# Cross-attention and FFN on one core: the first pair of heads scored in front of the last value tile, the first batch's transposes behind the next keys, the first keys chunk by chunk

## The chip, the cores and the metric

One Trainium2 chip, of which the kernel uses one core. The metric is the device time of one execution in microseconds (us); a run is compared with runs of the kernel before on the same chip.

## The reference

For each of B = 4 batches, x is 512 rows by 512 columns, and a context has T = 1601 rows of 512. The kernel computes, in float32:

```
q = layernorm(x) Wq^T + bq        k = ctx Wk^T + bk        v = ctx Wv^T + bv      (16 heads of 32)
p = softmax(clip(q k^T / sqrt(32), -50, 50)), masked rows of the context count as -50
a = LN((clip(rs, 0, 0.3) * (p v Wo^T + bo))) * gamma + beta;     x1 = x + a
y = fwht(layernorm(x1) * SU_ug) ; g = silu(y Wgate^T) * (y Wup^T) ; out = x1 + fwht(g * SU_dp) Wdown^T
```

## The kernel before

All instructions are written out per engine in hand-made order, with semaphores between the engines: each engine runs its own list, and a wait holds up everything behind it in that list. Large products are made from two fp32r parts of each operand, a high part (a copy, on ScalarE) and a low part (the difference, on VectorE), with three matmuls for each chunk of 128 rows of the contraction (`split_product`, L132).

**Stages.** `context` (L689) goes through the four batches. For each it first makes keys and values of the 1601 context rows in six pieces (`NP`, `FROM`: tiles of 128 rows, two per piece and three in the last, 13 in all), and then the scores and the attention, 52 steps. `ffn` follows. A piece is: load of the raw context (SyncE), its high part `split_hi` (L677, ScalarE) and low part `split_lo` (L682, VectorE); `keys` (L1187, TensorE), four tiles of 48 matmuls in all; `keys_hi` (L883) and `keys_lo` (L1030), which take each key tile out of its PSUM bank; `weighted` (L1196), the value products, 12 matmuls for each tile of context rows; `values_out` (L905), ScalarE's copy of a value tile into `vt`. Keys and values share the four banks `kv` = both halves of `sc[0]` and `sc[1]` (L711), so value tile i waits for the low part of key tile i, and the next piece's keys wait for the value copies.

**The first batch** also makes the queries of all four batches, one at a time (class `Queries`, L524): `norm` (L601, VectorE, with `root` on ScalarE), `transposes` (L625, TensorE, 16 matmuls of 128 columns), `rows_hi` and `rows_lo` (L576, L612), `project` (L634, 48 matmuls) and `query_hi` and `query_lo` (L585, L617). These use the other four banks, `banks` = both halves of `sc[2]`, `acc` and `tot` (L712). On TensorE (L1286 to L1305) piece p does keys(p), project(p - 1), weighted(p), transposes(p). On ScalarE (`first_piece` L953, `query_piece` L965) it does rows_hi, keys_hi, root, query_hi, values_out; on VectorE (L1097, L1107) rows_lo, keys_lo, norm, in piece 1 the first half of the butterflies of the down weights (`butterfly_ahead`, L489), query_lo, and in piece 1 the other half. SyncE loads (`first`, L784); GpSimd loads and stores the output, up and gate weights (L856 to L869) when the third and fourth transposes are done.

In front of everything TensorE waits (L1283) for the low parts of all four chunks of the key weights (`weights_lo`, L596). ScalarE makes the high part of the second context piece (L958) before it takes the first key tiles.

**The turn.** When the last value tile (tile 12, 65 rows) is copied into `vt`, `scores(b, 0)` (L1204) begins: 12 matmuls of 32 rows by 512 columns for four heads, three for each head, four heads side by side. Step i makes two pairs of heads, n = 2i and 2i + 1, each in a bank `sc[n % 3]` of two halves. `exps` (L930, ScalarE) takes the exponential of one pair at a time, `clips` (L1083, VectorE) bounds it, `values` (L1216) multiplies with `vt`, `sums` (L1228) adds up. `scores(b, i)` waits until all but the last exponential of the step before are done (L1207), since there are three banks for two pairs a step. The queries of batches 2 to 4 are loaded back from DRAM (`query`, L756) and must be there before the first scores; so must the low parts of the rotated rows (`rotated_lo`, L376), which use the banks of `sc[2]`. In the first batch, before the first exponential, ScalarE also waits for the stores of the output, up and gate weights (L1022, L1023), whose space the probabilities take.

## Time and profile before

| | us |
|---|---|
| median of three runs | 1475.78 (1474.55 to 1476.06) |
| the profiled execution, its own time | 1475.65 |
| span of its instructions | 1473.8 |
| TensorE busy | 1424.8 (97%) |
| VectorE busy | 1108.7 (75%) |
| ScalarE busy | 815.1 (55%) |
| mean granted TensorE clock | 0.989 of full speed |

The profiled execution's time is 1.85 us more than its span; times in timelines count from the span's start. PE is TensorE's matmuls, PEld its weight loads, DVE VectorE, ACT ScalarE, POOL GpSimd, SP SyncE. Busy times of matmuls run to their modelled ends, so that a row's length holds a tail beyond the start of the next instruction.

### The profile page before, as it was taken

Reading aid. Unit: us, or ns where it says so; the run is one execution under the profiler, and the core shown is the slowest. Engines: PE = TensorE matmul, PEld = TensorE weight load, DVE = VectorE, ACT = ScalarE, POOL = GpSimd, SP = SyncE. Lnnn points to the kernel's source line nnn. Section 1 sums busy time; section 2 is a strip of 40 time slices with the busy share of each in tenths; the row PEclk is TensorE's granted clock in tenths of the full one; section 3 lists DMA queues with packets and bytes.
Section 4 is the critical chain, followed back from the end, with each engine's and each line's share of the span. In section 5 each row is a group of like instructions: output and inputs, shape, how many; then the busy total and the mean of one; then the engine's idle time right before and its main releaser. Section 6 shows DMA issues by size and latency. Waiting matters only on the chain. (4 is left out here: it accounts for less than half of the span.)

```text
span 1473.8 us, 25109 instructions
## 1 busy us (share of the span) xinstructions
PE 1424.8 (97%) x10352; PEld 955.6 (65%) x10352; DVE 1108.7 (75%) x1657; ACT 815.1 (55%) x1018; POOL 88.9 (6%) x128
## 2 busy tenths in 40 slices
PE   5999999999999999999999999998999999999997
PEld 5887333688333688333588333576788888888886
DVE  5953899895899885799885799887765565656554
ACT  4343899535899635899634899534432333333330
POOL 1000000101000100000100000110010010000100
PEclk9999999999999999999999999999999999999999
DMA  8453000436100425100424500362345544455435
GB/s 270 149 189 143 9 10 10 148 104 203 79 17 10 138 84 192 36 17 10 137 79 179 226 16 10 95 236 84 143 150 203 189 173 146 157 205 178 171 143 171
DMA packets 54785, 180.91 MB, mean 123 GB/s; under 512 B 11168, under 2 KB 25760, under 8 KB 42384
## 3 DMA queue, kind: packets, MB, share of 16 engines
q1 hardware_dynamic: 39696, 116.08, 21.9%
q0 software_dynamic: 14976, 63.23, 12.7%
q8 instruction: 82, 1.34, 0.4%
q14 instruction: 31, 0.25, 0.1%
HBM read 111.97 MB, written 67.31 MB: 122 GB/s over the span
## 5 line engine op out<-in xcount | busy, mean ns | idle before, releaser
L944 ACT ACTIVATE cx_probs<-cx_sc,proj_mbias 128x1024 f32<-128x1024 f32 (+1 forms) x416 | 442.7, 1114 | 45.7 <-PE cx_sc L1211 38.1
L1089 DVE TENSOR_SCALAR cx_probs<-cx_probs 128x1024 f32<-128x1024 f32 (+1 forms) x416 | 269.9, 684 | 57.1 <-ACT cx_probs L944 55.7
L1051 DVE TENSOR_TENSOR cx_padd<-cx_probs,cx_probs 128x1024 f32<-128x1024 f32 x192 | 233.6, 1217 | 1.1 <-DVE cx_probs L1089 0.2
L1211 PEld LDWEIGHTS cx_sc<-cx_q,cx_kt 32*128 32x128 f32 (+1 forms) x2496 | 103.6, 183 | 198.3 <-ACT cx_probs L944 181.3
L1224 PE MATMUL cx_acc<-cx_probs,cx_vt 128*32 128x512 f32 (+1 forms) x1664 | 220.9, 603 | 3.7 <-DVE cx_probs L1089 3.7
L1211 PE MATMUL cx_sc<-cx_q,cx_kt 32*128 32x512 f32 (+1 forms) x2496 | 206.5, 433 | 14.5 <-ACT cx_probs L944 11.1
L136 PE MATMUL cx_sc<-proj_cs,proj_wk 128*128 128x256 f32 (+1 forms) x1152 | 149.1, 289 | 11.1 <-DVE proj_wk L599 11.1
L136 PEld LDWEIGHTS cx_sc<-proj_cs,proj_wk 128*128 128x128 f32 x1152 | 145.4, 190 | 15.3 <-issue 14.2
L136 PE MATMUL cx_sc<-proj_wv,proj_cs 128*128 128x512 f32 (+1 forms) x624 | 149.6, 396 | 1.2 <-DVE cx_kt L1036 1.2
L136 PE MATMUL ff_yp<-hand_wds,ff_held 128*128 128x512 f32 x624 | 147.9, 395 | 0.1
L1686 DVE TENSOR_TENSOR ff_x<-ff_yp,ff_x 128x512 f32<-128x512 f32 x128 | 85.6, 689 | 75.0 <-PE ff_yp L136 62.1
L136 PEld LDWEIGHTS ff_yp<-hand_wds,ff_held 128*128 128x128 f32 x624 | 117.1, 188 | 28.8 <-DVE ff_kept L1749 0.5
L136 PEld LDWEIGHTS cx_sc<-proj_wv,proj_cs 128*128 128x128 f32 (+1 forms) x624 | 113.6, 184 | 30.2 <-issue 1.8
L1236 PE MATMUL cx_tot<-cx_padd,cx_ones 128*32 128x256 f32 x1536 | 120.8, 390 | 0.0
L889 ACT ACTIVATE cx_kt<-cx_sc,proj_bk 128x256 fp32r<-128x256 f32 (+1 forms) x96 | 44.3, 480 | 70.6 <-PE cx_sc L136 70.4
L1224 PEld LDWEIGHTS cx_acc<-cx_probs,cx_vt 128*32 128x32 f32 (+1 forms) x1664 | 51.4, 110 | 48.8 <-DVE cx_probs L1089 11.5
L915 ACT ACTIVATE cx_vt<-cx_sc 128x512 f32<-128x512 f32 (+1 forms) x52 | 31.0, 597 | 93.5 <-PE cx_sc L136 93.5
L1634 ACT ACTIVATE ff_kept<-ff_gp 128x512 f32<-128x512 f32 x42 | 25.1, 599 | 96.1 <-PE ff_gp L136 96.1
L1236 PEld LDWEIGHTS cx_tot<-cx_padd,cx_ones 128*32 128x32 f32 x1536 | 31.8, 108 | 71.4 <-issue 47.7
L136 PE MATMUL ff_gp<-ff_t_t,ff_a 128*128 128x512 f32 x252 | 64.5, 391 | 0.0
L1749 DVE TENSOR_TENSOR ff_kept<-ff_yp,ff_kept 128x512 f32<-128x512 f32 x28 | 19.2, 687 | 52.9 <-PE ff_yp L136 52.9
L1036 DVE SCALAR_TENSOR_TENSOR cx_kt<-cx_sc,proj_bk,cx_kt 128x256 fp32r<-128x256 f32 (+1 forms) x96 | 43.4, 484 | 19.1 <-ACT cx_kt L889 18.9
(286 smaller groups left out, 1776.9 us busy)
## 6 DMA issues: line engine op xcount, KB each, us to landing
ff_x<-scr_x SPq DMA_DIRECT2D x32, 1024.0 KB, 5.0
scr_x<-ff_x SPq DMA_DIRECT2D x28, 1024.0 KB, 4.9
proj_raw<-in_ctxT SPq DMA_DIRECT2D x20, 512.0 KB, 4.9
hand_wds<-scr_wd POOLq DMA_DIRECT2D x7, 1024.0 KB, 10.1
scr_q<-cx_q SPq DMA_DIRECT2D x3, 2048.0 KB, 7.2
cx_wo<-scr_wo POOLq DMA_DIRECT2D x3, 2048.0 KB, 13.7
scr_xs<-cx_xs POOLq DMA_DIRECT2D x3, 2048.0 KB, 7.9
cx_q<-scr_q SPq DMA_DIRECT2D x3, 1536.0 KB, 10.9
```

The source lines that it names most:

```text
L136: last = nc.tensor.matmul(out, stationary(a, c), moving(z, c), start=first and n == 0, stop=final and n == len(parts) - 1, skip_group_chec ...
L889: nc.scalar.activation(kt[:, 0, c, t0:t0 + w], kv[c][:, 0:w], ACT.Identity, bias=bk[:, c:c + 1]).then_inc(k_hi, 1)
L915: nc.scalar.activation(vt[0:n, t], kv[t - FROM[p]][0:n], ACT.Copy).then_inc(v_out, 1)
L944: nc.scalar.activation(prob(N)[0:r], sc[n % NSC][0:r], ACT.Exp, bias=mbias[0:r, b, t:t + 1], scale=SCALE).then_inc(exp_done, 1)
L1036: nc.vector.scalar_tensor_tensor(kt[:, 1, c, t0:t0 + w], kv[c][:, 0:w], bk[:, c:c + 1], kt[:, 0, c, t0:t0 + w].bitcast(F32), ALU.add, ALU. ...
L1051: nc.vector.tensor_tensor(padd[z][(g * QP + j) % 2][:], prob(2 * i + z)[:], prob(2 * i + 2 + z)[:], ALU.add).then_inc(added[z], 1)
L1089: nc.vector.tensor_scalar(prob(N)[0:r], prob(N)[0:r], LOW, HIGH, ALU.max, ALU.min).then_inc(clip_done, 1)
L1211: last = nc.tensor.matmul(sc[(2 * i + h // 2) % NSC][0:r, h % 2], kt[own, z, c, t * P:t * P + r], q[own, y, c], start=n == 0, stop=n == 2)
L1224: last = nc.tensor.matmul(acc[h * HD:(h + 1) * HD], vt[0:r, t, (4 * c + h) * HD:(4 * c + h + 1) * HD], prob(N + h // 2)[0:r, h % 2], start ...
L1236: last = nc.tensor.matmul(tot[h * HD:(h + 1) * HD, cols], ones[:], padd[h // 2][(g * QP + j) % 2][:, h % 2, cols], start=j == 0 and half = ...
L1634: nc.scalar.activation(kept[k][:], part_banks[w][Sums.BANK[product]][:], ACT.Copy).then_inc(copied, 1)
L1686: nc.vector.tensor_tensor(x1[b % 2][:, j], bank[:], x1[b % 2][:, j], ALU.add).then_inc(y_read, 1)
```

## The change

It has three parts. *Turn:* before the last value tile of each batch TensorE makes the scores of the first pair of heads (`first_scores`, 6 matmuls), and ScalarE its exponential in front of the copy of that tile; the second pair's six matmuls follow the tile and no longer wait for its copy. The banks are renamed (`bank_of`), so that the first pair uses `sc[2]`, which is no key or value bank. The waits for rotated rows, queries and stores move along with it. *First batch:* TensorE's order in piece p becomes keys(p), transposes(p - 1), weighted(p), project(p - 1), and ScalarE's and VectorE's lists follow it. *Start:* the first key tile waits for the low part of the key weights chunk by chunk, and the high part of the second context piece moves behind the first key tiles on ScalarE.

```diff
@@ -747,6 +747,10 @@
+        def bank_of(n):
+            return sc[(n + NSC - 1) % NSC]
         def rows_of(t):
@@ -912,6 +916,12 @@
                             act.wait_ge(bias_done, 1)
+                        if t == TT - 1:
+                            if b == 0:
+                                act.wait_ge(wo_out, 16)
+                                act.wait_ge(ugw_out, 16)
+                                act.wait_ge(mask_done, 2)
+                            exp(b, 0)
                         nc.scalar.activation(vt[0:n, t], kv[t - FROM[p]][0:n], ACT.Copy).then_inc(v_out, 1)
...
                 def collect_values(b, c):
@@ -927,22 +937,26 @@
+                def exp(b, n):
+                    N = b * PAIRS_B + n
+                    t = n // 2 % TT
+                    r = rows_of(t)
+                    act.wait_ge(scores_done, N + 1)
+                    old = N // 2 - BUFS[n % 2]
+                    if old >= 0:
+                        act.wait_ge(values_done, old + 1)
+                        og, ot = divmod(old, TT)
+                        if ot < TT - 1:
+                            act.wait_ge(added[n % 2], og * QP + ot // 2 + 1)
+                        else:
+                            act.wait_ge(sums_done, og * SUMS + SINGLE)
+                    nc.scalar.activation(prob(N)[0:r], bank_of(n)[0:r], ACT.Exp, bias=mbias[0:r, b, t:t + 1],
+                                         scale=SCALE).then_inc(exp_done, 1)
                 def exps(b):
-                    for n in range(PAIRS_B):
-                        N = b * PAIRS_B + n
+                    for n in range(1, PAIRS_B):
                         c, t = divmod(n // 2, TT)
-                        r = rows_of(t)
-                        act.wait_ge(scores_done, N + 1)
-                        old = N // 2 - BUFS[n % 2]
-                        if old >= 0:
-                            act.wait_ge(values_done, old + 1)
-                            og, ot = divmod(old, TT)
-                            if ot < TT - 1:
-                                act.wait_ge(added[n % 2], og * QP + ot // 2 + 1)
-                            else:
-                                act.wait_ge(sums_done, og * SUMS + SINGLE)
-                        nc.scalar.activation(prob(N)[0:r], sc[n % NSC][0:r], ACT.Exp, bias=mbias[0:r, b, t:t + 1],
-                                             scale=SCALE).then_inc(exp_done, 1)
+                        exp(b, n)
                         if c and n % 2 == 0 and t == 1:
@@ -955,21 +969,21 @@
                     qu.weights_hi(nc, act, 1)
-                    context_hi(0, 1)
                     act.wait_ge(qu.consts_in, 3 * 16)
                     keys_hi(0, 0)
+                    context_hi(0, 1)
                     qu.weights_hi(nc, act, 2)
...
                 def query_piece(p):
+                    keys_hi(0, p)
                     qu.rows_hi(nc, act, p - 1)
-                    keys_hi(0, p)
                     if p < B:
                         qu.root(nc, act, p)
+                    values_out(0, p)
                     qu.query_hi(nc, act, p - 1)
-                    values_out(0, p)
                 def ready(b):
@@ -1019,9 +1033,6 @@
                     if b == 0:
-                        act.wait_ge(wo_out, 16)
-                        act.wait_ge(ugw_out, 16)
-                        act.wait_ge(mask_done, 2)
                         act.wait_ge(chain.rs_step, 4)
@@ -1106,8 +1117,8 @@
                 def query_piece(p):
+                    keys_lo(0, p)
                     qu.rows_lo(nc, dve, p - 1)
-                    keys_lo(0, p)
                     if p < B:
@@ -1190,6 +1201,13 @@
                             at_least(pe, v_out, b * TT + (FROM[p - 1] + c + 1 if p else 0))
+                        if n == 0 and c == 0:
+                            for chunk in range(HC):
+                                pe.wait_ge(qu.w_lo, chunk + 1)
+                                last = split_product(nc, kv[c][:, 0:w], lambda z, k: wk[:, z, chunk, c * P:(c + 1) * P],
+                                                     lambda z, k: cs[n % 2][:, z, chunk, 0:w], 1, chunk == 0, chunk == HC - 1)
+                            last.then_inc(k_done, 1)
+                            continue
                         split_product(nc, kv[c][:, 0:w], lambda z, k: wk[:, z, k, c * P:(c + 1) * P],
@@ -1197,21 +1215,33 @@
                         i, r = t - FROM[p], rows_of(t)
+                        if t == TT - 1:
+                            first_scores(b)
                         pe.wait_ge(k_lo, n * HC + i + 1)
...
-                def scores(b, i):
+                def scores(b, i, pairs=(0, 1)):
                     c, t = divmod(i, TT)
...
                     for n, (z, y) in enumerate(((0, 0), (0, 1), (1, 0))):
-                        for h in range(HC):
+                        for h in range(2 * pairs[0], 2 * pairs[-1] + 2):
                             own = slice(h * HD, (h + 1) * HD)
-                            last = nc.tensor.matmul(sc[(2 * i + h // 2) % NSC][0:r, h % 2], kt[own, z, c, t * P:t * P + r], q[own, y, c],
+                            last = nc.tensor.matmul(bank_of(2 * i + h // 2)[0:r, h % 2], kt[own, z, c, t * P:t * P + r], q[own, y, c],
                                                     start=n == 0, stop=n == 2)
...
                                 last.then_inc(scores_done, 1)
+                def first_scores(b):
+                    if b:
+                        pe.wait_ge(chain.xs_lo, b * HC)
+                        pe.wait_ge(q_in[0], b * 16)
+                    else:
+                        pe.wait_ge(qu.lo, B * HC)
+                    pe.wait_ge(k_lo, b * NP * HC + 1)
+                    scores(b, 0, (0,))
                 def values(b, i):
@@ -1280,7 +1310,6 @@
                 pe.wait_ge(pads, 1)
-                pe.wait_ge(qu.w_lo, HC)
                 for b in range(B):
@@ -1289,7 +1318,8 @@
                         if b == 0 and 1 <= p <= B:
-                            qu.project(nc, pe, p - 1)
+                            pe.wait_ge(qu.consts_in, 3 * 16)
+                            qu.transposes(nc, pe, p - 1)
                         if b == 0 and p == NP - 1:
@@ -1300,24 +1330,19 @@
                         weighted(b, p)
-                        if b == 0 and p < B:
-                            if p == 0:
-                                pe.wait_ge(qu.consts_in, 3 * 16)
-                            qu.transposes(nc, pe, p)
+                        if b == 0 and 1 <= p <= B:
+                            qu.project(nc, pe, p - 1)
                         if b:
...
                             chain.out_proj(nc, pe, room, b - 1)
-                    if b:
-                        pe.wait_ge(chain.xs_lo, b * HC)
-                        pe.wait_ge(q_in[0], b * 16)
-                    else:
+                    if b == 0:
                         pe.wait_ge(chain.rs_step, 4)
-                        pe.wait_ge(qu.lo, B * HC)
                     pe.wait_ge(k_lo, (b + 1) * NP * HC)
+                    pe.wait_ge(v_out, (b + 1) * TT - 1)
+                    scores(b, 0, (1,))
                     pe.wait_ge(v_out, (b + 1) * TT)
-                    scores(b, 0)
                     for i in range(STEPS):
...
```

## Rows read from the trace of the kernel before

**Rows 1.** The page: busy time of TensorE, its share of the span, and instructions.
```profile
PE 1424.8 (97%) x10352; PEld 955.6 (65%) x10352; DVE 1108.7 (75%) x1657; ACT 815.1 (55%) x1018; POOL 88.9 (6%) x128
```

**Rows 2.** Waits of TensorE: us in total, times, longest.
```profile
PE cx_sc L1211 <- ACT cx_probs L944: 11.1, 15, 1.3
```

**Rows 3.** Stretches: start:end, length, busy us of each engine, granted clock, DMA share, GB/s.
```profile
28.40:31.80 3.40, 3.24 (x16) 3.27 (x17) 2.74 (x6) 0.95 (x2) 0.00 (x0) 0.50 0.06 20
31.90:34.00 2.10, 2.10 (x20) 2.10 (x19) 2.06 (x4) 1.47 (x4) 1.25 (x2) 1.00 0.30 51
...
369.80:373.20 3.40, 1.32 (x17) 0.85 (x20) 0.31 (x1) 2.05 (x3) 0.00 (x0) 0.99 1.03 427
373.20:380.00 6.80, 5.62 (x40) 2.26 (x40) 4.89 (x7) 4.91 (x5) 0.00 (x0) 0.50 0.33 128
1018.30:1021.70 3.40, 1.99 (x9) 1.60 (x9) 2.67 (x3) 3.30 (x4) 0.00 (x0) 1.00 0.00 0
```

**Rows 4.** Timeline, first 21 us: start, length, engine, line, instructions [idle before].
```profile
8.52 2.49 DVE L599 TENSOR_TENSOR proj_wk<-cx_wraw,proj_wk 128x512 fp32r<-128x512 f32 x4 [0.49 <-ACT proj_wk L570]
...
11.11 7.51 PE L136 MATMUL cx_sc<-proj_cs,proj_wk 128*128 128x256 f32 x48 [11.11 <-DVE proj_wk L599]
...
17.62 1.06 ACT L680 ACTIVATE proj_cs<-proj_raw 128x1024 fp32r<-128x1024 f32 x1 [4.75 <-DMA proj_raw<-in_ctxT]
...
19.79 5.83 PE L136 MATMUL cx_sc<-proj_wv,proj_cs 128*128 128x512 f32 x24 [1.17 <-DVE cx_kt L1036]
...
20.74 1.21 DVE L685 TENSOR_TENSOR proj_cs<-proj_raw,proj_cs 128x1024 fp32r<-128x1024 f32 x1
```

**Rows 5.** Timeline, 25 to 32 us, first transposes and second keys.
```profile
25.37 1.07 ACT L915 ACTIVATE cx_vt<-cx_sc 128x512 f32<-128x512 f32 x2
...
28.56 1.94 PE L631 MATMUL cx_sc<-all_ident,cx_qxt 128*128 128x128 f32 x8 [2.94 <-DVE cx_qxt L609]
...
31.84 5.92 PE L136 MATMUL cx_sc<-proj_cs,proj_wk 128*128 128x256 f32 x48
```

**Rows 6.** Timeline, 38 to 63 us, VectorE's chain and the second projection.
```profile
38.71 2.46 DVE L605 BATCH_NORM_STATS2 cx_stats<-cx_qxt 128x6 f32<-128x512 f32 x4
...
50.18 1.41 DVE L620 SCALAR_TENSOR_TENSOR cx_q<-cx_sc,cx_bq,cx_q 128x512 fp32r<-128x512 f32 x2
...
57.67 2.29 DVE L483 TENSOR_TENSOR cx_ahead_fl<-cx_ahead_fl,cx_ws_dp 128x2048 f32<-128x2048 f32 x1
...
62.50 5.70 PE L136 MATMUL cx_sc<-cx_qxT,cx_wq 128*128 128x512 f32 x24 [0.91 <-DVE cx_qxT L615]
```

**Rows 7.** Timeline of the turn in the second batch.
```profile
369.89 0.59 ACT L915 ACTIVATE cx_vt<-cx_sc 65x512 f32<-65x512 f32 x1 [2.17 <-PE cx_sc L136]
370.74 0.98 PE L1211 MATMUL cx_sc<-cx_q,cx_kt 32*128 32x512 f32 x12 [0.89 <-ACT cx_vt L915]
371.75 2.12 ACT L944 ACTIVATE cx_probs<-cx_sc,proj_mbias 128x1024 f32<-128x1024 f32 x2 [1.26 <-PE cx_sc L1211]
372.91 1.48 PE L1211 MATMUL cx_sc<-cx_q,cx_kt 32*128 32x512 f32 x12 [1.19 <-ACT cx_probs L944]
...
377.15 1.94 PE L1224 MATMUL cx_acc<-cx_probs,cx_vt 128*32 128x512 f32 x8
...
381.63 0.74 PE L1211 MATMUL cx_sc<-cx_q,cx_kt 32*128 32x512 f32 x8 [0.21 <-ACT cx_probs L944]
```

**Rows 8.** Timeline in the middle of the first batch's attention.
```profile
260.16 0.97 PE L1211 MATMUL cx_sc<-cx_q,cx_kt 32*128 32x512 f32 x12
261.06 0.64 PE L1236 MATMUL cx_tot<-cx_padd,cx_ones 128*32 128x256 f32 x8
...
262.49 0.51 PE L1211 MATMUL cx_sc<-cx_q,cx_kt 32*128 32x512 f32 x4
```

**Rows 9.** DMA issues: size, and us to landing (the queries: issued at 359.95).
```profile
cx_q<-scr_q SPq DMA_DIRECT2D x1, 512.0 KB, 5.1
...
scr_ug<-cx_ugs POOLq DMA_DIRECT2D x1, 2048.0 KB, 8.3
```

## Prediction

> **What bounds the kernel now.** I read first the page's busy shares: TensorE is busy for 97% of the span [rows 1], so a gain has to come out of its 49 us of idle time, out of stretches at the lower clock, or out of fewer matmuls; the change takes no matmul away. Next I read whom TensorE waited for [rows 2]: the largest repeated wait is that of the score matmuls for an exponential, 11.1 us in 15 places. Then I read the granted clock by stretches [rows 3]: 0.50 of full speed, the 1.2 GHz level, between 28.4 and 31.8 and again between 373.2 and 380.0, and 1.00 at 31.9 to 34.0. TensorE had been idle for 2.94 us before the first of these [rows 5], and busy for only 1.32 of 3.40 us before the second; one lone gap of 1.41 us, in the stretch from 1018.3 with 1.99 us busy, left the clock at 1.00. So an idle place costs twice: its own time, and the half-speed matmuls behind it. The timelines of the two kinds of place that the change touches follow: the first 63 us [rows 4 to 6] and the turn from the projections to the scores, once per batch [rows 7].
>
> **The first batch.** *Keys chunk by chunk.* The key weights' low parts are four instructions in 2.49 us from 8.52, about 0.6 apart, and TensorE began at 11.11 after all four [rows 4]. With the first chunk, at 9.2, it can begin at 9.3, 1.8 us earlier; at half clock three matmuls take about 0.64 us, so the chunks keep ahead of it. But the 48 key matmuls took 7.51 us there and 5.92 us later [rows 4, 5]: the clock rose on the way. If it rises as soon after the first matmul as before, the end moves by the whole 1.8 us; if it rises at the same moment, by 1.0 (8 matmuls done early, at 0.12 each at full speed). I take 1.0: nothing in the rows ties the rise to the first matmul. Keys end at 17.6 instead of 18.6.
>
> *Key high parts before the next context.* ScalarE waited for the next context's load until 17.62, split it, and only then took the four key tiles, and TensorE waited 1.17 us for their low parts [rows 4]. Now the key tiles are taken as they end, and value products start at 17.6 instead of 19.79. The context split moves behind the last key tile, 18.2 to 19.2; its low part on VectorE starts at 19.25, because the low parts of keys are done by then, instead of at 20.74 [rows 4]. All of VectorE's normalisation, the root and the value copies behind it come 1.5 us earlier: the first copy ends near 24.45 (25.37 + 0.6 - 1.5 [rows 5]).
>
> *Transposes behind the next keys.* Before: idle 2.94, transposes from 28.56, next keys at 31.84 [rows 5]. Now value products end at 17.6 + 5.8 = 23.4, TensorE waits 1.2 us for the copy that frees the bank, keys run 24.6 to 30.4, and the transposes take 1.6 us (half of 3.28, since they ran at half clock) to 32.0; value products to 37.8, query projection (24 matmuls in 5.70 less the tail [rows 6], twice) to 48.7, next keys to 54.5, transposes to 56.2.
>
> There VectorE is late. It does in this order: low part of the query weights (2.49, ends at 29.3), low parts of the keys and the next context (to 32.2), rows' low parts (2.5, to 34.7), then from the statistics to the query's low parts 11.5 us (38.71 to 50.18 [rows 6]), 46.2. The fourth quarter of the projection is out at 48.8, its high and low part at 50.4. The second half of the down-weight butterflies then takes 7.1 us (four low parts of 0.7 from 50.18 end at 52.9, the last butterfly at 59.96 [rows 6]), to 57.5; the first low key part ends at 58.0. Value products start at 58.05, after 1.8 us of waiting. Before, the same count of work was left when the projection started at 62.50, after its own 0.91 us of waiting for these butterflies [rows 6]. One load could be late: the third context piece, issued behind the constants in both orders; I place it at 27.7, before any row shows its use, and each microsecond later costs one. The first batch gains 4.45 us. Bounds: 3.0 if the chunk waits bring nothing or that load is late, 6.2 if the clock rises earlier and VectorE's lateness vanishes.
>
> Further on in this batch projection and value products only change places, with TensorE as the bound in both orders. Moved with the transposes are the loads that GpSimd issues when they are done: the up and gate weights now start half a microsecond later and are wanted by ScalarE some 17 us after, so nothing waits. ScalarE starts the output weights right behind the last query high part, which ends when TensorE has just begun the last keys; before it was the last value copy, at the same point. So the store of the up and gate weights, 8.3 us [rows 9], keeps its place against TensorE.
>
> **The turn, four times.** Call T the end of the last value tile (369.86 in the second batch). Before: copy, 0.89 us idle, 12 score matmuls, idle 1.19 us for the first exponential, 12 more at falling clock, idle, and so on; the fifth score block starts at 381.63, T + 11.8 [rows 7]. The pattern stands four times: the same distance is 10.8 in the first batch, 11.8 and 11.6 in the third and fourth, 45.9 in all. From there exponentials run back to back and the rest of the batch is alike. The change puts 6 matmuls of the first block in front of the last tile. What does a half block cost? A whole block of 12 occupies 0.90 us before the next instruction starts [rows 8], in three rounds; the first four matmuls lie in 0.51 us together, and each alone takes that. So a round of two may last as long as a round of four: between 0.45 and 0.90; I take 0.90, as the rounds are the length. The Trainium skill (TensorE: Matmul & The Clock Gate, the part on packing small matmuls) says the same against this change: a matmul on 32 rows lasts as long as one on 128, and only matmuls in different row groups run beside each other. With 0.45 the sum would be 1.8 us better.
>
> New course, from P = T + 0.90: first exponential (1.06 each, two in 2.12 [rows 7]) done before P, under the last tile's products; second half block ends at P + 0.9, the copy at P + 0.6; second block of scores P + 0.9 to 1.85; second exponential to P + 2.05, third to 3.1; third block at P + 3.15 after 1.3 us of idle time; values; fourth block at P + 5.25; fifth at P + 7.35 = T + 8.25. Four times that is 33.0, so the turn gains 12.9 us, of which about 1 us per batch is the low clock that no longer comes. In front of the first exponential stand waits: the up and gate store lands about 0.6 to 1.2 us before it is wanted, with 1.5 us of slack more before the last copy is held up. The first scores want the new queries 2.7 us earlier: they landed at 359.95 + 5.1 = 365.1 and are wanted at 367.1 [rows 9]. The renamed banks keep their order and change no wait. SyncE's list is not touched; its other loads wait for the same events and are wanted 5 us or more after them.
>
> **Sum.** 4.45 + 12.9 = 17.35. The profiled execution took 1475.65 us (span 1473.8), the median is 1475.78; 1475.65 - 17.35 = 1458.3.
>
> **Rivals.** *The clock falls all the same* (0.27). Each turn still has 1.3 us of idle time and half-filled matmuls; before, a stretch with 1.32 of 3.40 us busy fell and one with 1.99 did not [rows 3], and the new one has about 2.0. Each fall costs 1.3 to 1.7 us (a score block 1.48 instead of 0.98, and near half of a value block of 1.94 [rows 7]); four give 1464.3, one or two 1461. The 1.8 us wait right after the transposes at 56.2 might do it too, for 1.7 us. The Trainium skill (same page, PE-mode transpose) holds that transposes do not count as activity, which would make that fall likely and give 1460. Here the trace disagrees: between 28.4 and 31.8 only transposes ran, and the clock was full right after [rows 3, 5].
>
> *The first batch gains nothing* (0.09): butterflies on VectorE already delayed TensorE by 0.91 us, and if its chain moves less than I think, everything in front of 62.5 is absorbed: 1462.8. For it, VectorE's own chain gains 1.5 us at first; against it, the removed idle time and half clock are TensorE's own.
>
> *The first scores become the new wait, and it is slower* (0.02): if the query load is late, first scores stand in front of the last value products, which then wait too. Every microsecond beyond the 2.0 of slack costs one in three batches; slower than before from 7.8 us later than 365.1; at 9 us late 1479. Against it: two of three loads were issued long before.
>
> *The exponential in front of the last copy does nothing* (0.03): if ScalarE gets there late, the copy is late by what was gained and the change is worth its first batch less four half blocks: 1474.8.
>
> **How the numbers follow.** The forecast has 0.59. A measurement of this kernel tells about 0.2% (3 us) from no change. Range: down to 1455.0 for cheap half blocks and an early clock, up to 1465.5 for a fall at every turn and some of the first batch absorbed. Only the last two rivals are not faster by over 0.2%: faster 0.95, same 0.03, slower 0.02.
>
> **What would show it.** First keys near 9.3; transposes behind keys with no wait of 2.9 us; a wait of 1 to 2 us for a low key part near 56; half blocks of about 0.9 us in front of the last value tile; granted clock 1.00 at all four turns; about 8.2 us from T to the fifth score block. Half clock at a turn, a wait for the query load, or an idle ScalarE before the first exponential would prove a step wrong.

## The result, and the profile after

Median of four runs 1466.24 us (1464.21 to 1468.02), beside 1475.92 for the kernel before on the same chip (1474.55 to 1477.35): a ratio of 0.9935 with a 95% interval of 0.992 to 0.995. The change gains 9.7 us where 17.35 were forecast, and the time lies 0.7 us above the range. The profiled execution was the longest of the four, 1468.02 us with a span of 1466.2 (1473.8 before). Its mean granted clock was 0.995, that of the other three 0.996 to 0.997; the falls of the clock that are counted below are those of this one execution.

I measured both traces at four points: first keys, last keys of the first batch, the distance of each turn, and the feed-forward network (the work from its first matmul on). Last keys start at 124.59 instead of 126.76: the first batch gained 2.2 us of the 4.45 forecast. From there to the start of the network, in which the four turns lie, it gained 6.4 of 12.9 (the turns' own distances, below, add up to 6.95). The feed-forward network took 530.8 us instead of 529.8. That is 7.6 of span.

The first 63 us of TensorE in the changed kernel, from its timeline (start, length, engine, line, instructions, idle before and what ended it), to hold against [rows 4, 5]:

```profile
9.44 7.16 PE L136 MATMUL cx_sc<-proj_cs,proj_wk 128*128 128x256 f32 x48 [9.44 <-DVE proj_wk L599]
16.44 5.76 PE L136 MATMUL cx_sc<-proj_wv,proj_cs 128*128 128x512 f32 x24
...
24.19 5.91 PE L136 MATMUL cx_sc<-proj_cs,proj_wk 128*128 128x256 f32 x48 [1.99 <-ACT cx_vt L925]
29.94 1.04 PE L631 MATMUL cx_sc<-all_ident,cx_qxt 128*128 128x128 f32 x8
...
58.63 7.40 PE L136 MATMUL cx_sc<-proj_wv,proj_cs 128*128 128x512 f32 x24 [2.95 <-DVE cx_kt L1047]
```

Keys start with the first chunk, value products follow without a gap and the 2.94 us in front of the transposes are gone. The wait that the prediction expected near 56 is there, but as 2.95 us instead of 1.8, and the clock falls behind it: 24 value products take 7.40 instead of some 5.8.

Now the turn in the second batch, same kind of view, with ScalarE's lines (ACT), to hold against [rows 7]:

```profile
364.46 0.97 PE L1231 MATMUL cx_sc<-cx_q,cx_kt 32*128 32x512 f32 x6
...
365.36 2.98 PE L136 MATMUL cx_sc<-proj_wv,proj_cs 128*65 128x512 f32 x12
368.28 0.97 PE L1231 MATMUL cx_sc<-cx_q,cx_kt 32*128 32x512 f32 x6
368.38 1.11 ACT L953 ACTIVATE cx_probs<-cx_sc,proj_mbias 128x1024 f32<-128x1024 f32 x1 [3.21 <-PE cx_sc L136]
369.40 0.58 ACT L925 ACTIVATE cx_vt<-cx_sc 65x512 f32<-65x512 f32 x1
370.03 0.97 PE L1231 MATMUL cx_sc<-cx_q,cx_kt 32*128 32x512 f32 x12 [0.79 <-ACT cx_vt L925]
372.20 0.97 PE L1231 MATMUL cx_sc<-cx_q,cx_kt 32*128 32x512 f32 x12 [1.20 <-ACT cx_probs L953]
...
376.56 0.98 PE L1231 MATMUL cx_sc<-cx_q,cx_kt 32*128 32x512 f32 x12 [0.20 <-ACT cx_probs L953]
```

The half block sits in front of the last tile and takes 0.90 us (364.46 to 365.36), and ScalarE is idle right behind it. But its first exponential does not start at 365.4. It starts at 368.38, after 3.21 us of idle time that the *value tile's products* ended (L136), not the scores (L1231). The copy stands behind it, so TensorE waits 0.79 us for the copy and then 1.20 for an exponential. The fifth block comes 8.21 us after the end of the last tile (P, 368.35), where the prediction had 7.35.

The stretches of the granted clock (start:end, length, busy us of TensorE, weight load, VectorE, ScalarE and GpSimd, granted clock, DMA share, GB/s), for the wait near 56 and for the four turns:

```profile
56.70:60.10 3.40, 1.47 (x6) 1.24 (x7) 3.40 (x5) 0.00 (x0) 0.56 (x1) 1.00 0.90 305
60.10:63.50 3.40, 3.40 (x9) 2.63 (x8) 3.40 (x8) 0.00 (x0) 0.00 (x0) 0.50 0.96 371
145.40:148.80 3.40, 1.40 (x18) 0.79 (x20) 1.70 (x3) 3.34 (x5) 0.00 (x0) 1.00 0.02 5
148.90:152.20 3.30, 3.30 (x24) 0.98 (x20) 2.84 (x5) 2.68 (x3) 0.00 (x0) 0.50 0.01 2
370.70:374.10 3.40, 2.20 (x28) 0.65 (x20) 2.30 (x4) 3.28 (x4) 0.00 (x0) 1.00 0.56 211
588.30:591.70 3.40, 1.42 (x20) 0.91 (x24) 1.87 (x3) 3.34 (x5) 0.00 (x0) 1.00 0.04 15
807.60:811.00 3.40, 1.52 (x20) 0.99 (x24) 1.96 (x3) 3.34 (x5) 0.00 (x0) 1.00 1.00 330
811.10:814.40 3.30, 3.30 (x24) 1.04 (x20) 2.98 (x5) 2.42 (x3) 0.00 (x0) 0.50 1.02 432
```

At the turns of batches one and four the clock fell to the 1.2 GHz level behind the two gaps; at those of two and three it did not, with the same instructions. The busy time does not tell them apart: 1.40 and 1.52 us in front of a fall, 1.42 in the third batch without one. The distances from the last tile to the fifth score block say the same: 9.48, 8.21, 8.20, 9.46. A fall at a turn costs 1.26 us. Before, the clock had fallen at all four turns, for 3.4 us in the first batch and for 6.8 in the others (two more of these stretches of the kernel before):

```profile
151.30:154.70 3.40, 3.40 (x24) 1.02 (x24) 2.89 (x5) 2.79 (x3) 0.00 (x0) 0.50 0.01 2
...
816.90:823.70 6.80, 5.62 (x40) 2.09 (x40) 5.50 (x7) 4.67 (x6) 0.00 (x0) 0.50 1.01 428
```

Now each fall lasts about 3.4 us.

TensorE's waits (us in total, times, longest) in place of [rows 2]:

```profile
PE cx_sc L1231 <- ACT cx_probs L953: 6.9, 14, 1.2
...
PE cx_sc L1231 <- ACT cx_vt L925: 3.2, 4, 0.8
PE cx_sc L136 <- DVE cx_kt L1047: 2.9, 1, 2.9
```

11.1 us of waiting for exponentials became 6.9. The wait for the four last copies, which the change was to hide, is still 3.2 us in all; before it was 3.4.

### The profile page after: what moved, and what is told of

It reads as the page before. It is cut to its first block and busy times, and to the rows that moved or that the text cites. A ratio compares the mean times of both kernels' runs of the same rounds, so it can differ in the third digit from the quotient of the medians.

```text
span 1466.2 us, 25120 instructions
## 1 busy us (share of the span) xinstructions
PE 1422.5 (97%) x10352; PEld 954.0 (65%) x10352; DVE 1107.8 (76%) x1657; ACT 814.4 (56%) x1018; POOL 88.9 (6%) x128
## 5 line engine op out<-in xcount | busy, mean ns | idle before, releaser
L1231 PEld LDWEIGHTS cx_sc<-cx_q,cx_kt 32*128 32x128 f32 (+1 forms) x2496 | 103.3, 180 | 193.1 <-ACT cx_probs L953 173.2
L1231 PE MATMUL cx_sc<-cx_q,cx_kt 32*128 32x512 f32 (+1 forms) x2496 | 206.4, 426 | 10.1 <-ACT cx_probs L953 6.9
L136 PE MATMUL cx_sc<-proj_cs,proj_wk 128*128 128x256 f32 (+1 forms) x1152 | 148.4, 288 | 11.4 <-DVE proj_wk L599 9.4
L136 PEld LDWEIGHTS cx_sc<-proj_cs,proj_wk 128*128 128x128 f32 x1152 | 145.2, 190 | 16.2 <-issue 15.0
L136 PE MATMUL cx_sc<-proj_wv,proj_cs 128*128 128x512 f32 (+1 forms) x624 | 152.3, 399 | 2.9 <-DVE cx_kt L1047 2.9
L136 PE MATMUL ff_yp<-hand_wds,ff_held 128*128 128x512 f32 x624 | 147.9, 395 | 0.1
L136 PEld LDWEIGHTS ff_yp<-hand_wds,ff_held 128*128 128x128 f32 x624 | 117.1, 188 | 28.9 <-DVE ff_kept L1774 0.5
L136 PEld LDWEIGHTS cx_sc<-proj_wv,proj_cs 128*128 128x128 f32 (+1 forms) x624 | 114.2, 186 | 33.1 <-DVE cx_kt L1047 3.2
L136 PE MATMUL ff_gp<-ff_t_t,ff_a 128*128 128x512 f32 x252 | 64.5, 391 | 0.0
```

The lines of the kernel that those rows point to most:

```text
L136: last = nc.tensor.matmul(out, stationary(a, c), moving(z, c), start=first and n == 0, stop=final and n == len(parts) - 1, skip_group_chec ...
L1231: last = nc.tensor.matmul(bank_of(2 * i + h // 2)[0:r, h % 2], kt[own, z, c, t * P:t * P + r], q[own, y, c], start=n == 0, stop=n == 2)
```

## The experiments

**Theory A**: the missing part is lost at two places. ScalarE's wait for the last tile's products stands in front of the first exponential, so the exponential cannot run under that tile, and the two gaps that remain sometimes bring the clock down. In the first batch, the second half of the butterflies, which VectorE does before the next piece's first low key part, delays TensorE near 56, and the clock falls there too. **Rivals**: the half block or the packed scores are dearer than read; the falls alone are the loss; the first batch's gain was absorbed elsewhere; the difference is scatter of the profiled execution.

The table gives each kernel's profiled execution: start of the last keys of the first batch, the four turn distances (end of the last tile to the fifth score block), the length of the feed-forward network, then the median of its runs and its ratio to the kernel before, run beside it on the same chip, with the 95% interval. **Bold** is a turn or a network in which the clock fell.

| kernel | last keys | turns | network | median | ratio |
|---|---|---|---|---|---|
| before | 126.76 | **10.82** **11.77** **11.76** **11.55** | 529.8 | 1475.92 | |
| after | 124.59 | **9.48** 8.21 8.20 **9.46** | 530.8 | 1466.24 | 0.9935 [0.992, 0.995] |
| after_again | 123.92 | **9.47** 8.23 8.20 **9.47** | 530.8 | 1466.61 | 0.9935 [0.9921, 0.9948] |
| e1_exp_first | 122.92 | 7.53 7.47 7.46 7.45 | 529.2 | 1462.63 | 0.992 [0.9905, 0.9934] |
| e2_turn_alone | 126.85 | 8.20 **9.46** 8.20 8.21 | 529.0 | 1468.72 | 0.9964 [0.995, 0.9977] |
| e3_no_turn | 123.36 | **11.72** **10.70** **11.67** **11.78** | 528.6 | 1471.82 | 0.9982 [0.9971, 0.9993] |
| e4_butterflies | 120.36 | **9.46** 8.24 8.21 8.21 | **531.9** | 1462.71 | 0.9921 [0.9906, 0.9936] |
| e5_start_alone | 125.29 | **10.82** **11.77** 9.56 **11.68** | 529.4 | 1472.75 | 0.9981 [0.9968, 0.9994] |
| e7_all_three | 119.71 | **8.78** 7.46 7.47 7.45 | 529.6 | 1457.71 | 0.9881 [0.9864, 0.9897] |
| e8_exp_butterflies | 120.28 | 7.53 7.46 7.46 7.45 | 529.9 | 1460.29 | 0.9896 [0.9878, 0.9914] |
| e10_filler | 123.83 | 8.35 8.36 8.35 8.32 | 527.9 | 1462.34 | 0.9912 [0.9896, 0.9928] |
| e11_all_filler | 120.1 | 7.52 7.52 7.53 7.54 | 528.0 | 1455.84 | 0.9865 [0.9844, 0.9885] |
| e12_load_early | 122.19 | 8.19 8.20 **9.46** 8.21 | 529.7 | 1464.11 | 0.9921 [0.9906, 0.9936] |
| e13_all_early | 119.74 | 7.53 7.46 7.45 7.45 | 529.1 | 1458.17 | 0.9884 [0.9863, 0.9906] |

Each distance is measured from P; from the old T, in front of the half block, 0.90 us more is to be added for all kernels with the new turn.

The intervals of e1, e4, e10 and e12 overlap with those of the changed kernel, so what one of these edits is worth is read from the traces and not from the whole time; those of e7, e8, e11 and e13 lie below that of the second run of the changed kernel.

### The wait in front of the first exponential

`e1_exp_first` takes the exponential from behind the wait for the tile's products:

```diff
 for t in range(FROM[p], END[p]):
     n = rows_of(t)
+    if t == TT - 1:
+        ...
+        exp(b, 0)
     act.wait_ge(v_done, b * TT + t + 1)
     ...
-    if t == TT - 1:
-        ...
-        exp(b, 0)
```

> The changed kernel, with the first exponential (and its waits) put in front of ScalarE's wait for the last value tile's products, behind which the change has it. Theory A (that wait is what held the exponential back by a whole value tile, and it explains most of the gap to the prediction): the first exponential starts about 1 us after the first half block of scores and ends before the last value tile does; the fifth score block starts 7.4 us after the second half block instead of 8.3 (9.5 where the clock falls); the clock falls at fewer turns; 4 to 8 us less than the changed kernel, 1459 to 1462. Theory B (half blocks, the copy and the clock set the turn anyway): the exponential is early but the third score block is not, under 1.5 us less, 1465 to 1466.

The first batch's turn, from its timeline:

```profile
139.10 0.97 PE L1231 MATMUL cx_sc<-cx_q,cx_kt 32*128 32x512 f32 x6
140.00 2.99 PE L136 MATMUL cx_sc<-proj_wv,proj_cs 128*65 128x512 f32 x12
140.19 1.12 ACT L953 ACTIVATE cx_probs<-cx_sc,proj_mbias 128x1024 f32<-128x1024 f32 x1 [0.38 <-PE cx_sc L1231]
142.92 1.71 PE L1231 MATMUL cx_sc<-cx_q,cx_kt 32*128 32x512 f32 x18
143.02 0.59 ACT L925 ACTIVATE cx_vt<-cx_sc 65x512 f32<-65x512 f32 x1 [1.72 <-PE cx_sc L136]
...
146.16 0.98 PE L1231 MATMUL cx_sc<-cx_q,cx_kt 32*128 32x512 f32 x12 [1.53 <-ACT cx_probs L953]
```

This is the course that the prediction wrote down: exponential under the tile, ended by its own scores (L1231), the copy right behind the tile, 18 score matmuls in one piece, one gap of 1.53 us (1.3 forecast). The distance is 7.45 to 7.53 at all four turns and the clock stays up. So 0.75 us per turn (8.21 to 7.46) is the wait itself, and no turn fell here with the second gap gone. All other terms of the turn are as read. The whole time is less clear: the profiled execution took 1459.63 us, but it was the fastest of five, and the median of 1462.63 lies just above the 1459 to 1462 that I had given.

`e2_turn_alone` keeps the turn and undoes the edits of the first batch; `e3_no_turn` is the reverse.

> Only the change's turn; start and first batch as in the kernel before. Theory A: the turn gains 0.4, 2.7, 2.7 and 1.2 us in the profiled run, about 7 us together, so 1469. Theory B (the first batch made the gain, the turn about nothing): 1473 to 1476.

> Only the change's start and first batch; scores, banks and first exponential as in the kernel before. Theory A: the last keys of the first batch start 2 us earlier than before (124.6 instead of 126.8), 1473 to 1474. If start and first batch are worth the 4.5 us of the prediction and something takes them back at the turn: 1471.

The two differ from the kernel before that ran beside them (1474.27) by 5.6 and 2.5 us. Together 8.0, beside the 9.7 for both and 8.6 in the second run of the changed kernel (1475.2 to 1466.61), differences within the width of these intervals: no sign that one part hides the other. In e3 the wait near 56 is 2.78 us and the clock stays up behind it, so its last keys start at 123.36, earlier than the 124.6 expected. One of four turns fell in the first, and each clean one still took 8.20, so falls alone are not the loss.

### The wait near 56

`e4_butterflies` moves the second half of the butterflies on VectorE from the end of `query_piece(1)` to behind the rows' low parts at `p == 2`; nothing else changes.

> The changed kernel, with the second half of the down-weight butterflies on VectorE moved from the end of piece 1 to behind the rows' low parts of piece 2. Theory C (the 2.95 us wait for a key low part at 55.7, and the half clock after it, are these butterflies): no wait over 0.5 us there, no fall of the clock near 60, the last keys of the first batch start at 120 instead of 124.6, 4 us less than the changed kernel, 1462. Rival (the load of the third context piece is what is late): the wait stays above 1.5 us, less than 1.5 us gained.

The wait is gone. TensorE's two lines there and VectorE's, from its timeline:

```profile
55.61 0.60 PE L631 MATMUL cx_tot<-all_ident,cx_qxt 128*128 128x128 f32 x4
...
55.97 5.84 PE L136 MATMUL cx_sc<-proj_wv,proj_cs 128*128 128x512 f32 x24
...
58.03 2.35 DVE L487 TENSOR_TENSOR cx_ahead_spare<-cx_ahead_fl 128x1024 f32<-128x1024 f32 x2
```

Value products start right behind the transposes and run at full speed; last keys start at 120.36, 4.2 us ahead of the changed kernel's first profile and 3.6 ahead of its second. `e8_exp_butterflies` joins this edit and that of e1:

> The changed kernel with both edits: first exponential in front of the wait, butterflies behind the rows' low parts. If the two losses are separate and of the size of the profiles (the turn 0.9 us four times and 2.2 us where the clock fell, the first batch 2.95 us and 1.7 us of half clock): 1458 to 1460, the prediction's time. If they overlap: 1461 to 1462, no better than either alone.

It has the turns of e1 and the keys of e4 in one kernel, and its median of 1460.29 lies just above the 1458 to 1460 expected. `e7_all_three` adds a third: ScalarE takes the first value copies (`values_out(0, 0)`) before the root of the query's normalisation, and the 1.99 us wait near 24 is gone. In its place stands a new one of 0.52 us at 30.88, for a low key part, as the rival had said:

> As the run before, and ScalarE makes the first two value copies ahead of the root of the normalisation, so that TensorE doesn't wait 2 us for them at 22 us. If that wait is worth its length: 1 to 2 us less than with two edits. Rival (the load of the third context piece lands at 31 whatever TensorE does, so the wait only moves to a key's low part near 33): within 0.7 us of it, with a new wait there.

Its 1457.71 is close to the 1458.3 that the prediction had for the change itself, but by another way: the last keys start at 119.71, 2.6 us earlier than the 122.3 of the forecast. In the profile of e7 the clock fell once, behind a single gap, where e8 with the same turn kept it. Stretches of e7, and then the like stretch of e8:

```profile
140.20:143.50 3.30, 1.77 (x24) 1.02 (x26) 1.27 (x2) 2.93 (x4) 0.00 (x0) 1.00 0.00 0
143.60:147.00 3.40, 3.40 (x28) 1.05 (x20) 3.08 (x6) 2.43 (x3) 0.00 (x0) 0.50 0.01 2
```

```profile
140.40:143.80 3.40, 1.87 (x22) 1.14 (x26) 1.00 (x2) 3.03 (x4) 0.00 (x0) 1.00 0.00 0
```

### The first load, and the chunks alone

`e5_start_alone` is the kernel before with the chunk waits and the keys taken ahead of the next context, transposes and turn as they were.

> The kernel before with the change's start alone (keys chunk by chunk, key high parts ahead of the next context). TensorE starts keys at 9.3 and value products 2.2 to 3 us earlier than 19.79. If the start is worth what reaches the last keys of the first batch: they start 0.5 to 2 us earlier than 126.8, 1474. Rival (the queries' normalisation and the butterflies on VectorE absorb it): last keys within 0.3 us of 126.8, same time.

```profile
27.01 1.76 PE L631 MATMUL cx_sc<-all_ident,cx_qxt 128*128 128x128 f32 x8 [4.09 <-DVE cx_qxt L609]
```

The first keys start at 9.74 and value products at 17.16, 2.6 us earlier than before, but TensorE then waits 4.09 us for the transposes' rows instead of 2.94: 1.5 us is left at the last keys. The earlier start needs the transposes moved as well. The median is 3.1 us below the kernel before, more than these 1.5, but one turn of the old kind stayed at full clock in this profile, and the interval is wide.

This kernel has the old turn, and its third one shows what that costs when the clock stays up:

```profile
590.76 0.97 PE L1226 MATMUL cx_sc<-cx_q,cx_kt 32*128 32x512 f32 x12 [0.88 <-ACT cx_vt L919]
592.94 0.98 PE L1226 MATMUL cx_sc<-cx_q,cx_kt 32*128 32x512 f32 x12 [1.20 <-ACT cx_probs L947]
595.10 0.98 PE L1226 MATMUL cx_sc<-cx_q,cx_kt 32*128 32x512 f32 x12 [1.19 <-ACT cx_probs L947]
...
599.44 0.97 PE L1226 MATMUL cx_sc<-cx_q,cx_kt 32*128 32x512 f32 x12 [0.19 <-ACT cx_probs L947]
```

Here the score blocks last 0.97 to 0.98 us, where one in [rows 7] takes 1.48, and the distance is 9.56 us. So a fall of 6.8 us in the old turn cost 2.1 to 2.2 us in this kernel (11.77, 11.68) and one of 3.4 us cost 1.26 (10.82), the same as in the new turn. Over the four turns of the kernel before that is 7.7 us (45.9 less four times 9.56), where the prediction had "about 1 us per batch". Against this clean turn the changed kernel's clean one (8.21 and the half block's 0.90, 9.11) gains 0.45 us, e1's (7.46 + 0.90) 1.2. As built, the change owes most of its gain at the turns, some 5 of 6.95 us, to falls that come less often and last less long.

`e12_load_early` is the changed kernel with SyncE's load of the third context piece issued in front of the constants, since the load landed at 31.1 where the prediction had 27.7:

```diff
+proj.load(sp, io, 0, 2)
 chain.load_consts(sp, io)
-proj.load(sp, io, 0, 2)
```

> The changed kernel with the load of the third context piece ahead of the seven constant loads in SyncE's list. Theory E (this load, landing at 31.1 instead of the 27.7 that I assumed, makes VectorE's chain 2.2 us late): it lands at 26 to 28, the statistics of the second batch's rows start near 34.7 instead of 36.9, and the wait of 1.8 to 2.95 us near 56 falls by 0.6 us or more; up to 2 us less than the changed kernel (a fall of the clock less). Rival (the query projection on TensorE is what VectorE waits for, so the chain meets it anyway): the wait near 56 stays as it is, same time.

```profile
57.76 1.43 PE L136 MATMUL cx_sc<-proj_wv,proj_cs 128*128 128x512 f32 x5 [1.67 <-DVE cx_kt L1047]
...
34.35 2.47 DVE L605 BATCH_NORM_STATS2 cx_stats<-cx_qxt 128x6 f32<-128x512 f32 x4
...
49.50 0.75 DVE L620 SCALAR_TENSOR_TENSOR cx_q<-cx_tot,cx_bq,cx_q 128x512 fp32r<-128x512 f32 x1 [1.03 <-ACT cx_q L592]
```

The load now lands 4.9 us after its issue instead of 7.8, and the statistics start at 34.35 instead of 36.94 (34.7 forecast). What that is worth at TensorE depends on where the load lands otherwise, and that differs between executions of the same instructions. ScalarE takes the piece at 31.14 in the first profile of the changed kernel, at 30.99 in e1 and at 31.43 in e3, and the wait near 56 is 2.95, 2.92 and 2.78 us. It takes it at 29.96 in the second profile and at 29.82 in e10, and the wait is 1.79 and 1.80. In e12 it takes it at 27.72, and the wait is 1.67: VectorE then waits for the projection's quarters further on. The value products start at 58.63, 58.50 and 58.95 in the first three, at 57.98 and 57.86 in the next two and at 57.76 in e12. So taking the piece at 31 instead of 30 costs about 0.8 us, and taking it earlier still gains 0.1 to 0.2. Here the clock stayed up, and the last keys start at 122.19; the prediction's sum had been 122.3.

`e13_all_early` adds this load to e7. It is within the measurement of e7:

> The kernel with the three edits and the early load of the third context piece. Its TensorE has only 0.52 and 0.20 us of waiting left between 20 and 60 us, so at most 0.7 us less than 1457.7, not to be told from no change.

### The gap filled

`e10_filler` leaves the changed kernel's order as it is and fills the turn's two gaps with matmuls whose result nobody reads (3 in the first, 5 in the second, on data at hand):

```diff
+def filler(count):
+    for k in range(count):
+        nc.tensor.matmul(acc[:], kt[:, 0, 0, 0:P], kt[:, 0, 1, 0:S], start=True, stop=True)
 scores(b, 0, (1,))
+filler(3)
 pe.wait_ge(v_out, (b + 1) * TT)
 ...
+if i == 0:
+    filler(5)
```

> The changed kernel with 3 and 5 matmuls without use (128 rows by 512 columns, into the bank of the sums of products, which the first values overwrite) in the two gaps of each turn, 0.65 and 1.1 us. Theory D (the idle gaps pull the clock down at some turns): clock 1.00 at all four turns, the fifth score block about 8.4 us after the second half block at every turn, 1 to 4 us less than the changed kernel and less spread. Rival (the clock falls for another reason or its falls cost little there): same time or up to 1 us more, and the clock still falls.

```profile
366.39 0.97 PE L1231 MATMUL cx_sc<-cx_q,cx_kt 32*128 32x512 f32 x6
367.29 0.98 PE L1239 MATMUL cx_acc<-cx_kt 128*128 128x512 f32 x3
368.19 0.97 PE L1231 MATMUL cx_sc<-cx_q,cx_kt 32*128 32x512 f32 x12
369.10 1.43 PE L1239 MATMUL cx_acc<-cx_kt 128*128 128x512 f32 x5
370.46 0.97 PE L1231 MATMUL cx_sc<-cx_q,cx_kt 32*128 32x512 f32 x12
374.82 0.97 PE L1231 MATMUL cx_sc<-cx_q,cx_kt 32*128 32x512 f32 x12 [0.21 <-ACT cx_probs L953]
```

The filler (L1239) lies exactly in the old gaps, and all four turns take 8.32 to 8.36: 0.15 more than a clean one, 1.1 less than a fallen one. That is 2.0 us less over the four turns than in the second profile of the changed kernel. The whole times differ by more, 1462.34 against 1466.61 for the medians and 5.0 us between the profiled executions, but 2.9 of these 5.0 lie in the feed-forward network, which the filler does not touch. So 2.0 us is what the filler is shown to be worth. `e11_all_filler` is e7 with six such matmuls in its one gap:

> The kernel with the three edits (1457.7) and 6 matmuls without use in the one gap of 1.45 us that is left in each turn. If falls of the clock still happen there in some executions (one of four turns in its profile): clock 1.00 at all turns, 0 to 1 us less. Rival (the filler delays the third score block by its tail): up to 0.5 us more.

A turn costs 0.07 more than a clean one in e7, and in this profile the clock falls at none; over four turns that is 1.05 us less than in e7, where it fell at one. Its median, 1455.84 (1455.49 to 1456.45), is the best of the study, 20 us below the kernel before, but its interval and that of e7 overlap.

`after_again` is the changed kernel once more, unchanged, to tell scatter from cause:

> The changed kernel itself, beside the kernels that start from it, because its first four runs spread over 3.8 us. If its spread is the clock falling at some turns and not at others: the median within 2 us of 1466, and in this profile another number of falls than two turns and the wait near 56 us.

The falls come at the same two turns as in the first profile, so another number of them, which I had expected, did not show, and the spread of the runs stays unexplained. The wait near 56 is 1.79 this time, exactly the one forecast, and the clock falls behind it all the same.

## Why the prediction was wrong, point by point

**The step that failed**: "first exponential (1.06 each, two in 2.12) done before P, under the last tile's products". The exponential is written inside the loop over value tiles, behind `act.wait_ge(v_done, b * TT + t + 1)`. An engine works its list in order, so ScalarE waits for the last tile's products before it comes to an exponential that needs only the scores. The half block was out 3.0 us before the exponential began. I had listed the waits that the change puts in front of the exponential (output weights, store, mask) and asked for their slack, and left out the one that the loop already had. "An idle ScalarE before the first exponential" was named as a sign of a wrong step, and it came: 3.21 us. The price is 0.75 us at each turn, 3.0 in all (e1, clean turns), and it leaves two gaps in place of one.

**The falls of the clock at the turns**: the largest rival (0.27) priced a fall at 1.3 to 1.7 us; it measures 1.26. In the changed kernel two of four turns fell, in both profiles, so 2.5 us. They are part of the same failed step in that nearly all disappear once the exponential moves: none of eight turns in e1 and e8, one of four in e7.

**The turn's other terms** held. The half block costs 0.90, not 0.45: a round of two matmuls lasts as long as one of four, as the prediction had taken it. The Trainium skill (TensorE: Matmul & The Clock Gate, Why this matters for your kernels, the row on small-K matmuls) says that a single matmul on 32 rows takes the time of one on 128. The trace goes with it: three rounds of two take 0.90 us, as three rounds of four do. The gap left in e1 is 1.46 to 1.53 (1.3 forecast), the distance 7.45 to 7.53 (7.35). No wait for queries or rows showed at the first scores, and the rival of a late query load and that of an exponential that does nothing are out.

**The first batch**: the order of events was right, two sizes were not. e12, with no fall and the load early, reaches the last keys at 122.19 (122.3 forecast). In the changed kernel they start at 124.59 and 123.92. The larger part is the clock, which falls behind the wait near 56: 24 products take 1.6 us longer. That was in the text too, as something that "might" happen, for 1.7 us, and was not in the sum. The smaller part is the load of the third context piece, placed at 27.7 and taken at 31.1 in the profiled execution: value products start at 58.63 where the sum had 58.05. The prediction said that each microsecond later costs one; 3.4 us cost 0.9 (58.63 against 57.76 in e12).

The Trainium skill's rule that transposes do not count as activity (TensorE: Matmul & The Clock Gate, PE-mode transpose) was weighed at this place as the reason for a fall. Such a fall came, but behind waits of 1.79, 1.80 and 2.95 us, and not behind 1.67, 2.78 and 2.92 us in e12, e3 and e1, with the transposes in front of the wait each time; the rule does not tell these apart. The other terms: first keys at 9.44 (9.3); value products at 16.44 in the first profile and 17.67 in the second (17.6), as the clock rises at another moment; the wait near 24 1.99 and 1.28 us (1.2).

**The remainder**: the feed-forward network, with the same instructions in every kernel, took 527.9 to 531.9 us, 1.0 more in the changed kernel than before. Of this 1.0, TensorE's wait at the up product makes 0.7 (1.8 us against 1.1), and 0.3 lie behind the last matmul. The wait goes roughly with the landing of the output weights:

```profile
ff_wo<-scr_wo POOLq DMA_DIRECT2D x1, 2048.0 KB, 16.4
```

and in the kernel with the filler:

```profile
ff_wo<-scr_wo POOLq DMA_DIRECT2D x1, 2048.0 KB, 14.9
```

TensorE's wait at the up product was 1.8 us in the first and 0.3 in the second. e4 has the longest network, with a landing of 15.7 and the same wait of 1.8 us, because in it the clock fell behind this wait:

```profile
960.70:964.10 3.40, 3.40 (x9) 2.67 (x9) 1.28 (x3) 0.00 (x0) 0.00 (x0) 0.50 1.02 405
```

Without e4 the networks lie between 527.9 and 530.8 us. The change touches none of this; I take it as scatter, and why the load's time varies was not tried.

**Added up**, for the profiled execution, as losses against the forecast: 3.0 for the exponential behind the wait, 2.5 for two falls at turns, 0.4 for a turn that takes 7.46 even without either (7.35), 2.3 in the first batch (1.6 for the fall near 56, 0.6 for the late load), and 1.0 in the network: 9.2 of the 9.75 between 7.6 and 17.35. The 0.5 left lies between the turns, where no row names it. The median of the changed kernel misses the forecast by 7.9 us and not by 9.75, since the profiled execution was the slowest. The kernel with only the failed step mended is e1. Its profiled execution has clean turns, the last keys at 122.92 and 1459.63 us, 1.3 above the forecast, but its median is 4.3 above; what its other executions lost was not profiled. That e7 comes within 0.6 us of the forecast is luck, since it gains 2.6 us in the first batch by edits that the forecast did not have.

**The chances**: a fall somewhere had 0.27, and it happened three times in each profile of the changed kernel. The rows had shown a fall behind a stretch with 1.32 busy us and none behind one with 1.99; the turns of the changed kernel stood at 1.40 and 1.52 where the clock fell and at 1.42 where it did not, so no such comparison would have settled it. The range was made from cases in which every edit does in full what it says.

## What to carry to other kernels

When an instruction is moved earlier on its engine, read every wait between its new place and the work before it, the ones that were already in the loop first: what it needs itself may have been done for long, and the engine still stands at somebody else's semaphore. In a place with several short gaps, count what the clock does to the work behind them as part of the sum and not as a rival. If a gap can't be closed, matmuls without use in it may pay; they cost 0.07 to 0.15 us per turn here against 1.26 for a fall. And when two profiles are compared, look first at what the change does not touch: the network alone moved by up to 2.9 us between executions here, as much as an edit.

## What the runs showed of the hardware

- Whether the clock falls at a turn is not settled by the instructions alone: identical turns of one kernel fell and did not fall in the same execution (9.48 and 8.21), and with a single gap of about 1.5 us the clock fell at one of sixteen turns in e1, e7, e8 and e13. With gaps of 0.79 and 1.20 us and a 0.97 us block between them it fell at two of four turns, twice, and at one of four in e2, e4 and e12. With the gaps filled, none of eight fell. What decides between like turns stays open.
- Near 56, behind the same work, the clock fell after waits of 1.79, 1.80 (e10) and 2.95 us, and not after 1.67, 2.78 and 2.92 us. At the up product of the network it fell after a wait of 1.84 us in e4 and not after 1.77 in the changed kernel. The length of the gap alone does not decide.
- A fall of 3.4 us cost 1.26 us at a turn, the old (10.82 against 9.56) and the new (9.47 against 8.21), and 1.6 near 56; one of 6.8 us cost 2.1 to 2.2.
- 32 matmuls that compute nothing, eight in the gaps of each turn, made the four turns 2.0 us shorter (35.4 to 33.4 in all).
- The same 512 KB load landed 6.4 to 7.8 us after its issue behind the constants (6.7 and 7.8 in two executions of the same kernel) and 4.9 us in front of them.
